# Layer 2's router in a four-layer transformer kernel: one choice over all tokens, or one over chunks 0 to 2 and one over chunk 3

## What is computed

```python
def _fused_branch(Q_side, K_side, V, W, U, b, router_w1, router_b1, router_w2, router_b2, expert_bias):
    xV = jnp.einsum('btd,kdr->btkr', Q_side, V)
    yW = jnp.einsum('btd,kdr->btkr', K_side, W)
    cum_yW = jnp.cumsum(yW, axis=1)
    prod = xV * cum_yW
    h = jax.nn.gelu(Q_side @ router_w1.T + router_b1, approximate=False)
    logits = h @ router_w2.T + router_b2 + expert_bias
    weights = jax.nn.softmax(logits, axis=-1)
    out = jnp.einsum('btkr,kdr->btd', prod * weights[..., None], U)
    out = out + weights @ b
    n_valid = jnp.arange(1, Q_side.shape[1] + 1, dtype=Q_side.dtype)
    return out / n_valid[None, :, None]
```

## Time and profile before

| what | value |
|---|---|
| median of three runs | 1520.68 us |
| the profiled execution's own time | 1519.66 us |
| its span in the trace | 1517.4 us |
| TensorE (PE) busy | 1364.9 us, 90% |
| TensorE weight load (PEld) busy | 995.3 us, 66% |
| VectorE (DVE) busy | 994.9 us, 66% |
| ScalarE (ACT) busy | 945.8 us, 62% |
| GpSimd (POOL) busy | 745.1 us, 49% |

### The profile page before, as it was taken

One profiled execution on the slowest core, in us unless ns is written; L12 is line 12 of the kernel. 1 busy time (PEld: TensorE's weight loads), 2 busy tenths in 40 slices (PEclk: granted clock), 3 DMA queues, 4 the chain that ended last, 5 costly groups with the idle time before them and its releaser, 6 DMA issues. The chain is left out here.

```text
span 1517.4 us, 29689 instructions
## 1 busy us (share of the span) xinstructions
PE 1364.9 (90%) x9561; PEld 995.3 (66%) x9561; DVE 994.9 (66%) x2345; ACT 945.8 (62%) x1946; POOL 745.1 (49%) x764
## 2 busy tenths in 40 slices
PE   3699996998797788999998899899999999999986
PEld 2355555987374566777776577567777777777765
DVE  2677864777566767777776456577767667777651
ACT  1488784687565646666665356566767667666652
POOL 2355544110373215666564667365656656465541
PEclk8799997999799989999999899899999999999997
DMA  3500000000000210000000100000000000000002
GB/s 119 123 1 0 0 2 28 2 1 1 1 1 1 87 42 1 1 1 0 0 0 1 35 0 2 0 1 1 1 0 0 0 0 0 0 0 0 1 2 84
DMA packets 29772, 20.54 MB, mean 14 GB/s; under 512 B 9489, under 2 KB 26744, under 8 KB 29688
## 3 DMA queue, kind: packets, MB, share of 16 engines
q1 hardware_dynamic: 28536, 18.95, 4.3%
q10 hardware_dynamic: 1152, 0.52, 0.1%
HBM read 18.42 MB, written 1.05 MB: 13 GB/s over the span
## 5 line engine op out<-in xcount | busy, mean ns | idle before, releaser
L1958 POOL TENSOR_TENSOR arena<-arena,l3a_rinv 128x512 f32<-128x512 f32 x256 | 258.9, 1040 | 200.4 <-DVE l3a_rinv L2262 199.9
L2170 ACT ACTIVATE arena<-l3a_scores_ps,l3a_nmax 128x512 f32<-128x512 f32 x256 | 174.7, 685 | 118.3 <-DVE l3a_nmax L2256 118.3
L1958 POOL TENSOR_TENSOR arena<-arena,l2a_rinv 128x512 f32<-128x512 f32 x128 | 129.5, 1040 | 99.2 <-DVE l2a_rinv L2262 98.4
L2256 DVE TENSOR_REDUCE l3a_nmax<-l3a_scores_ps 128x2 f32<-128x1024 f32 x128 | 155.9, 1219 | 20.4 <-PE l3a_scores_ps L2014 20.4
L816 ACT ACTIVATE l0a_prob<-l0a_scores_ps,l0a_k_scale 128x1024 f32<-128x1024 f32 x128 | 135.4, 1113 | 40.5 <-PE l0a_scores_ps L712 39.9
L2027 PE MATMUL l3a_turned_ps<-const,arena 128*128 128x128 f32 x1024 | 145.0, 274 | 2.3 <-DVE z_lo L292 1.2
L2268 DVE COPY l3a_probT<-l3a_turned_ps 128x512 f32<-128x512 f32 x128 | 88.5, 691 | 80.8 <-PE l3a_turned_ps L2027 80.7
L2027 PEld LDWEIGHTS l3a_turned_ps<-const,arena 128*128 128x128 f32 x1024 | 119.2, 141 | 25.7 <-issue 8.9
L2038 PE MATMUL l3a_work_ps<-l3a_probT,l3a_v 128*64 128x256 f32 x1024 | 124.6, 385 | 2.6 <-DVE x_tokens L2283 1.6
L2170 ACT ACTIVATE arena<-l2a_scores_ps,l2a_nmax 128x512 f32<-128x512 f32 x128 | 87.4, 685 | 56.7 <-DVE l2a_nmax L2256 56.7
L2038 PEld LDWEIGHTS l3a_work_ps<-l3a_probT,l3a_v 128*64 128x64 f32 x1024 | 69.5, 136 | 52.0 <-issue 23.5
(11 more groups left out here) (692 smaller groups left out, 3581.7 us busy)
## 6 DMA issues: line engine op xcount, KB each, us to landing
l1f_w<-in_L_ffn_w SPq DMA_DIRECT2D x16, 256.0 KB, 2.7
load_ctx_rows<-in_ctx SPq DMA_DIRECT2D x1, 1536.0 KB, 7.5
l3f_experts_w<-in_L_ffn_W SPq DMA_DIRECT2D x24, 64.0 KB, 1.9
w_l_w<-in_L_ffn_W SPq DMA_DIRECT2D x1, 1024.0 KB
out_x<-x_tokens SPq DMA_DIRECT2D x8, 128.0 KB, 1.9
const<-in_constants SPq DMA_DIRECT2D x1, 589.0 KB
w_l_wo<-in_L_xattn_Wo SPq DMA_DIRECT2D x1, 512.0 KB
l0f_raw_f<-in_L_xattn_W_f SPq DMA_DIRECT2D x1, 512.0 KB, 4.1
```

What stands on the lines that cost most here:

```text
L1958: e.tensor_tensor(prob[n][:, :], prob[n][:, :], bcast(rinv[:, n:n + 1], [P, S]), ALU.mult).then_inc(m.prob_ready, 1)
L2170: e.activation(prob[at][:, :], bank(u), ACT.Exp, bias=nmax[:, at:at + 1], accum_out=rsum[:, at:at + 1]).then_inc(m.exp_ready, 1)
L2256: e.tensor_reduce(nmax[:, at:at + 2], sps[:, i * 1024:(i + 1) * 1024].rearrange("p (h k) -> p h k", h=2), AX.X, ALU.max, negate=True).then ...
```

## The change

The logits of chunks 0 to 2 go to one PSUM bank and those of chunk 3 to another. The tiles of the choice get a dimension for the branch, so that a part is a range of tiles of both branches: part 0 is tiles 0 to 11, part 1 tiles 12 to 15. The eleven VectorE instructions of the choice are issued once for each part, on 192 and 64 values per partition where they had 256 (24 and 8 where they had 32), and the Exp of ScalarE is issued twice. VectorE's order is: shift(0), total(0), shift(1), place_weights(0), total(1), place_weights(1). TensorE's wait before the turns is now in the loop: 4 for turns 0 to 2, and 8 for turn 3. `red` becomes four tiles. Nothing of the arithmetic is changed.

```diff
+            PARTS = [(0, TILES - CT), (TILES - CT, TILES)]
-            lps = s.ps("logits")
+            lps = [s.ps(f"logits{i}") for i in range(2)]
...
+                    part = c // (TURNS - 1)
                     for i in range(CT):
                         at = (r * TILES + CT * c + i) * E
-                        last = e.matmul(lps[:, at:at + E], hT[r][c % 2][:, i * P:(i + 1) * P], g.l2_rw2T[:, :],
+                        last = e.matmul(lps[part][:, at:at + E], hT[r][c % 2][:, i * P:(i + 1) * P], g.l2_rw2T[:, :],
...
-                e.wait_ge(m.w_st_ready, 4)
                 e.wait_ge(m.ident_ready, 1)
                 e.wait_ge(m.zeroed, 1)
                 for n in range(TURNS):
+                    e.wait_ge(m.w_st_ready, 8 if n == TURNS - 1 else 4)
...
-                e.wait_ge(m.shifted_ready, 1)
-                e.activation(ex[:, :, :], shifted[:, :, :], ACT.Exp).then_inc(m.ex_ready, 1)
+                for n, (lo, hi) in enumerate(PARTS):
+                    e.wait_ge(m.shifted_ready, n + 1)
+                    e.activation(ex[:, :, lo:hi, :], shifted[:, :, lo:hi, :], ACT.Exp).then_inc(m.ex_ready, 1)
...
+                def shift(n):
+                    lo, hi = PARTS[n]
+                    e.wait_ge(m.logits_ready, 2 * (hi // CT))
+                    then(e.tensor_tensor(biased[:, :, lo:hi, :],
+                                         lps[n][:, 0:2 * TILES * E].rearrange("p (r i e) -> p r i e", r=2, e=E)[:, :, lo:hi, :],
+                                         bcast(bias[:, :].unsqueeze(1).unsqueeze(1), shape(n)), ALU.add))
+                    then(e.tensor_reduce(red[0][:, :, lo:hi], biased[:, :, lo:hi, :], AX.X, ALU.max))
+                    e.tensor_tensor(shifted[:, :, lo:hi, :], biased[:, :, lo:hi, :],
+                                    bcast(red[0][:, :, lo:hi].unsqueeze(3), shape(n)), ALU.subtract).then_inc(m.shifted_ready, 1)
+
+                def total(n):
+                    lo, hi = PARTS[n]
+                    e.wait_ge(m.ex_ready, n + 1)
+                    then(e.tensor_reduce(red[1][:, :, lo:hi], ex[:, :, lo:hi, :], AX.X, ALU.add))
+                    then(e.reciprocal(red[2][:, :, lo:hi], red[1][:, :, lo:hi]))
+
+                def place_weights(n):
+                    lo, hi = PARTS[n]
+                    then(e.tensor_tensor(red[3][:, :, lo:hi], red[2][:, :, lo:hi], scale[:, :, lo:hi], ALU.mult))
+                    then(e.tensor_tensor(w[:, :, lo:hi, :], ex[:, :, lo:hi, :], bcast(red[3][:, :, lo:hi].unsqueeze(3), shape(n)), ALU.mult))
+                    twice = [bcast(w[:, r, lo:hi, :].unsqueeze(2), [P, hi - lo, 2, E]) for r in range(2)]
+                    for r in range(2):
+                        e.tensor_copy(places_of[:, lo:hi, :, r, 0, :], twice[r]).then_inc(m.w_st_ready, 1)
+                    for r in range(2):
+                        e.wait_ge(m.w_st_ready, 4 * n + r + 1)
+                        e.tensor_tensor(places_of[:, lo:hi, :, r, 1, :], twice[r], places_of[:, lo:hi, :, r, 0, :],
+                                        ALU.subtract).then_inc(m.w_st_ready, 1)
+
                 e.wait_ge(m.scale_ready, 2)
+                shift(0)
+                total(0)
+                shift(1)
+                place_weights(0)
+                total(1)
+                place_weights(1)
```

More of the change, by code:

```diff
@@ L2770, in l2_ffn @@
             zero = s.sb("zero", [P, D])
-            G = 2 * TILES
-            scale = s.sb("scale", [P, G])
-            red = s.sb("red", [P, 4, G])
+            PARTS = [(0, TILES - CT), (TILES - CT, TILES)]
+            scale = s.sb("scale", [P, 2, TILES])
+            red = [s.sb(f"red{k}", [P, 2, TILES]) for k in range(4)]
             bias = s.sb("bias", [P, E])
[L2775 to L2778, removed]
+            biased = s.sb("biased", [P, 2, TILES, E])
+            shifted = s.sb("shifted", [P, 2, TILES, E])
+            ex = s.sb("ex", [P, 2, TILES, E])
+            w = s.sb("w", [P, 2, TILES, E])
             w_st = g.z_hi[:, :].rearrange("p (i q) -> p i q", q=P)
@@ L2935, in _ @@
                 then(e.tensor_tensor(bias[:, :], g.l2_rb2[:, :], g.l2_eb[:, :], ALU.add))
-                places = scale[:, :].rearrange("p (r b i) -> p r b i", r=2, i=TPB)
+                places = scale[:, :, :].rearrange("p r (b i) -> p r b i", i=TPB)
                 by_place = bcast(g.const[:, C_INVN:C_INVN + TPB].unsqueeze(1), [P, B, TPB])
@@ L2957, in _ @@
                 e.tensor_tensor(b_parts[low, :], g.l2_b[low, :], b_parts[low, :], ALU.subtract).then_inc(m.b_ready, 1)
[L2959 to L2964, removed]
@@ L2965, in _ @@
-                e.tensor_tensor(shifted[:, :, :], logits, bcast(red[:, 0, :].unsqueeze(2), full),
-                                ALU.subtract).then_inc(m.shifted_ready, 1)
-                e.wait_ge(m.ex_ready, 1)
-                e.wait_ge(m.scale_ready, 2)
[L2969 to L2981, removed]
+                places_of = w_st[:, :, 0:ROWS].rearrange("p i (twice r part k) -> p i twice r part k", twice=2, r=2, part=2)
@@ new lines, in shape @@
+                def shape(n):
+                    return [P, 2, PARTS[n][1] - PARTS[n][0], E]
+                def shift(n):
[7 more added lines that the diff above has]
+                                    bcast(red[0][:, :, lo:hi].unsqueeze(3), shape(n)), ALU.subtract).then_inc(m.shifted_ready, 1)
```

## The result

| kernel | median (us) | runs | ratio to before, 95% interval |
|---|---|---|---|
| before | 1521.2 | 8 | |
| changed | 1516.84 (1514.97 to 1518.97) | 8 | 0.9973 [0.9963, 0.9984] |
| changed, once more | 1517.29 | 12 | 0.9981 [0.9973, 0.9990] |

The change makes the kernel faster. By the ratio it is 0.27% (4.1 us) in the first comparison and 0.19% (2.9 us) in the second, larger one; the medians themselves lie 4.4 us (1516.84 against 1521.2) and 3.2 us (1517.29 against 1520.51) apart. The forecast was 1518.9 us with a range from 1516.9; the first median lies 0.06 us under that range, the second in it. The profiled execution took 1516.78 us with a span of 1514.9 us, 2.5 us less than the span of before.

What follows compares the result with a forecast made beforehand. Bound: the serial chain of logits, choice and turns, with TensorE idle 4.60 us. 1.78 us of head start less 0.05 us of longer chain gives 1.73 us: 1520.68 - 1.73 = 1518.9 us, range 1516.9 to 1521.0.

Steps and rivals of the forecast that it cites:

- Head start: Router's choice on VectorE: part 0 needs no logits of chunk 3, so it begins 1.78 us earlier, 863.12 for 864.90.
- Lengths of the pieces: Choice's smaller operations: 0.158 us plus 1.04 ns per value, so 0.36 us for 192 values and 0.225 for 64.
- pieces cost as much as wholes: Choice on VectorE: a fixed cost sets instruction time, part 1 makes turn 3 0.55 us late, 1521.2 us; chance 5%.
- Hand-over to TensorE: From part 0's last subtraction on VectorE to the first turn on TensorE: 0.05 us.
- Part 1: Second part of the choice on VectorE: done at 869.16, 0.11 us before turn 3 wants it.
- What goes through to the experts: From the choice through the turns to the experts: 1.78 us less 0.05 us of longer chain, 1.73 us earlier.
- The clock: TensorE in turns and experts: falls before the turns, 5.1 us at the lower level stay; no part in the sum.
- my first rival: TensorE's clock doesn't fall before the turns; experts' first 12 matmuls take 2.4 us less: 1516.3 us; chance 6%.
- my third: Experts' start on TensorE: the clock returns 7.2 us later, costing 3.4 us: 1522.3 us; chance 4%.
- what would show it: Profile signs: TensorE idle about 2.9 us before the turns; experts' first stretch at 0.50 differing from 5.1 us refutes the clock step.
- The chances: Whole kernel: faster by over 0.2% (under 1517.6 us) 0.15, slower by over 0.2% 0.03, no difference that can be told 0.82.
- the forecast's own range: Whole kernel: 1517.4 to 1520.6 us, from 1.4 us scatter either side and part 1 up to 0.5 us late.

Runs made afterwards that it cites:

- The experiment on that wait: Changed kernel with TensorE's wait for part 0 put ahead of the two other waits before the turns: 1516.74 us (12 runs), ratio 0.9975.
- the split without head start: Changed kernel with both parts of the choice waiting for all eight groups of logits: 1520.39 us (11 runs), ratio 0.9998.

## Why the prediction was wrong in size and right in direction

- **Head start** (1.78 us forecast): part 0 starts 1.68 us before the last logits end, where the whole started 0.04 us after it: 1.72. Right.
- **Lengths of the pieces**: 0.36, 0.22, 0.30 and 0.20 us for the reciprocal, 0.36 and 0.26 for the Exp; all within 0.01 us of the line through 256 and 32 values. Part 0's chain up to its last subtraction took 4.52 us (863.00 to 867.52), forecast 4.57. Right; the rival "pieces cost as much as wholes" is out.
- **Hand-over to TensorE** (0.05 forecast): 0.26 us. The step failed in a detail. I wrote that TensorE's added waits are already met, and looked at turns 1 and 2; what cost 0.2 us was the order of the waits before turn 0. The experiment on that wait shows it.
- **Part 1**: done at 868.98, 0.3 us before turn 3 wanted it (its weight load starts at 869.27). Right, and TensorE has no pause there.
- **What goes through to the experts**: 1.73 forecast, 1.54 measured (9.53 to 7.99; 1.50 of it at the turns).
- **The clock.** This is the step that failed: "So I give the clock no part in the sum". The clock did fall before the turns, as I had said, and neither my first rival (it stays up) nor my third (it comes back later) came. But I then took the 5.1 us at the lower level at the experts' start as a fixed cost that moves along with the stage. The runs showed that the return doesn't move along: it came 14.6 us after the last logits for starts of 9.5 and of 11.2 us, and 11.2 us after them for the changed kernel's start of 8.0, so that the start of the stage had 3.18 us at the lower level instead of 5.17, and its end 3.41 instead of 5.25. The stage got 1.57 us shorter on top of the forecast, nearly as much as the change itself gave. The trace of before had two signs of it that I read past: the end of the experts' stage, which was at the lower level too and which I never looked at, and the number itself, 5.1 us, that I could have asked what it hung on. The section on what would show it named just this row, as something that would "hide or double" the gain, and then gave it no weight in the range.
- **The chances**: faster by over 0.2% had 0.15. It came, at 0.27% and, in the second comparison, 0.19%, at the edge of the bound. That the second median lies in the range is luck: the forecast's own range ended at 1517.4, and it went down to 1516.9 only for the rivals, none of which came. With the clock's part in, the sum would have been 1.5 + 1.6 = 3.1 us, just at the bound of 0.2%, and the chances of faster and same should have been about even.

Left open: why the return takes the moments it takes, and whether they would stand elsewhere if the block before were changed; no run here moved the logits themselves. The 0.8 us that the first pair of profiles loses behind this stage can't be put down to the change: over the nine profiles without unread matmuls that last part takes 549.4 to 552.6 us (551.5 and 551.7 in the two of the changed kernel, 551.9 in the split without head start), and the kernel before has one profile alone, with 550.7.

## What to carry to other kernels

A microsecond taken from, or added to, a gap in front of a busy TensorE stage need not be worth a microsecond: here 1.5 us less gave 3.1, 1.7 us more gave back 3.0 to 3.4 on one kernel and cost nothing on the other. Before pricing such a change, cut the stages behind it where the granted clock changes, at both of their ends, take the price per microsecond at the lower level from those rows, and ask for each stretch whether its end moves along. When a small edit brings twice what its instructions can explain, shift the unchanged kernel by the same time, with dummy work or by leaving work out, before crediting the edit; and write first the wait that will end last.

## What the runs showed of the hardware

The clock returned at few moments in relation to the program, while the work was moved by 3.4 us (in the kernels without unread matmuls, starts from 7.8 to 11.2 us and returns at 11.1 to 11.7 or at 14.5 to 15.0 us). The Trainium skill (TensorE: Matmul & The Clock Gate, section Part 1: The HAM clock gate) says that the monitor runs freely and isn't reset by the kernel; that the return doesn't follow the work agrees with it. It also says that the moment of a change varies by 500 ns to either side from run to run for that reason. In the fourteen profiles of this study the clock fell 0.84 to 1.46 us after the last logits (1.05 in the kernel before, 1.46 in the changed one with its wait first), a spread of 0.6 us, which agrees. That is little against the 3.5 us between the two groups of returns, so the effect is reproducible and shows in the medians.

Unread matmuls of 512 columns in TensorE's idle time brought the clock back 4.3 to 4.5 us after the last logits, where it had come back after 11.1 to 15.0. And a wait that stands as an instruction of its own on TensorE costs about 0.1 us when it is the last to end: in the changed kernel the two waits and the weight load behind them started at 867.56, 867.67 and 867.75.
